# One Mamba-and-FFN block on one core: the first up and gate tile of a round ahead of the transposition of y's first half, in the last chunk and the tail

## Chip, core and metric

One core of a Trainium2 chip runs the whole kernel. The metric is the device time of one execution in microseconds (us); lower is better. The engines are TensorE (PE), VectorE (DVE), ScalarE (ACT), GpSimd (POOL) and SyncE (SP, which issues the DMAs here). Each runs its own list of instructions in order, and they meet at semaphores.

## What is computed

4096 tokens (4 sequences of 1024), 512 wide, float32:

```python
x = x + layernorm(mamba(layernorm(x)))
x = x + layernorm(ffn(layernorm(x)))

# mamba: DI = 1024 channels, 16 states, dt rank 128
hidden, gate = split(x @ W_in + b_in)
conv  = silu(causal_conv4(hidden) + conv_b)
dt, B, C = split(conv @ W_x)
delta = softplus(dt @ W_dt + b_dt)
h[t]  = exp(delta[t] * A) * h[t-1] + delta[t] * conv[t] * B[t]
y[t]  = sum over the 16 states of h[t] * C[t]
y     = (y + conv * d_param) * silu(gate)
out   = y @ W_out + b_out

# ffn: 2048 inner; fwht is a Hadamard transform with signs and scales
z   = silu(fwht(x) @ W_gate) * (fwht(x) @ W_up)
out = fwht(z) @ W_down
```

## The kernel before

The tokens are cut into NCH = 16 chunks of T = 256. The Hadamard transforms are folded into the FFN weights during the first chunks. The program is a pipeline over rounds c = 0 to 18. In round c four or five chunks are in work: `cur` = c is scanned, `front` = c + 1 gets its in_proj, convolution and delta, `back` = c - 1 has its y turned, gated and projected, `ff` = c - 2 goes through the FFN, and `fold` = c - 3 finishes it. A chunk that does not exist is `None`: at c = 15 there is no `front`, and at c = 16 neither `front` nor `cur`. At c = 17 there is no `back` either.

A round has 32 slots, two (tb = 0, 1) for each of the 16 states n. Every engine has its own hand-written `slot` or `in_slot` function, which lists what it issues in slot k; `run` calls it for all c and k. The order of work on an engine is thus written out by hand, and semaphores do the rest.

What PE issues around the change, in `in_slot` (L779):

- slot 0: `turn_h(back, 15, 0)`, then `up_gate(fold, 15)`;
- slot 1: `turn_f(ff)` (transposes of the FFN's input; ACT and DVE split the result into `fxT_hi` and `fxT_lo`), at c = 16 a `down`, then `turn_h(back, 15, 1)`;
- slot 2: `turn_y(back, 0)`, `up_gate(ff, 0)`, and with a `cur` `turn_h(cur, 0, 0)`;
- slot 3: `turn_y(back, 1)`, and with a `cur` `turn_h(cur, 0, 1)` and a `down`;
- from slot 4 on: one `turn_h` in each slot (with a `cur`), `up_gate` in the even ones, and `down` (FFN down projection, L742), `out_proj` of `back` (L703) and `in_proj` of the gate (L651) between them.

`turn_h` (L628, transposes L633), `turn_f` (L610, L615), `turn_x` and `turn_y` (L618, transposes L625) all write the one PSUM tile `hT`. Each starts with `begin_t` (L575), which waits until the use before it in the list `T_SEQ` (L185) has been read out: for a turn_h that is DVE's addition to `acc` (`add_h`, L1183; L1190 for n = 0, L1193 otherwise), for a turn_y DVE's `skip` (L1196; four instructions at L1200 which add `hT` to `conv`, `y_skip`). `turn_y(back, 0)` also waits for the last `acc` of `back`.

`up_gate(j, ft)` (L709, 24 matmuls at L726) makes the gate and up rows of FFN tile ft of chunk j. It waits for its weights (`ug_in` or `ug_kept`), for ft = 0 for `fx_lo`, and for the tile before it in the same PSUM bank:

```python
def gate_up_bank(no):
    return da[0] if no >= SPARE and no % 2 else pF
def bank_users(no):
    return no - 1 if no > SPARE else no
# in up_gate, no = j * HT + ft, HT = 16, SPARE = 224:
    if no:
        pe.wait_ge(p_done, bank_users(no))
```

`p_done` is counted up by the second instruction of DVE's `silu_up` (L1210; L1215 and L1217). The tiles of the rounds meant here are no = 208 (c = 15) and no = 224 (c = 16), and both use `pF`.

DVE's list around it, in its own `in_slot` (L1232), for a round with a `cur`:

- slot 1: scan(0, 2), `f_low` (`fxT_lo`), scan(0, 3), `add_h(back, 15, 1)`, `silu_up(fold, 15)`;
- slot 2: scan(1, 0), `skip(back, 0)`, scan(1, 1), `add_h(cur, 0, 0)`;
- slot 3: scan(1, 2), `skip(back, 1)`, scan(1, 3), `add_h(cur, 0, 1)`, `silu_up(ff, 0)`.

Here scan(n, q) is quarter q of state n (L1180). Without a `cur` the scans and the additions of `cur` are not there. ACT makes each quarter's `decay` (L986) when the scan two quarters back is done, the tanh (L1010), and once a round `gate_silu` (L1003), each use of which loads two activation tables, its own and then that of the next `decay`. POOL makes `dbx` (L1362), the low part of the product (`prod_lo`, L1426), the gating (L1410) and the last addition of a chunk (`xr`, L1436); SP's `store_out` waits for the latter, and SP's later loads stand behind it.

Of the kernel before, what the change touches and what calls it, by code (L numbers as in the profile page):

```python
# [35 lines left out]
def fused_block(nc, x, W, scratch_bc, scratch_ug, scratch_wd, out):  # L36
# [31 lines left out]
    with ctx:  # L68
# [108 lines left out]
        def chunk(c):  # L177

            return c if 0 <= c < NCH else None
# [7 lines left out]
        for c in range(LAST + 1):  # L187
            cur, front, back, ff = chunk(c), chunk(c + 1), chunk(c - 1), chunk(c - 2)
# [30 lines left out]
# [8 lines that stand above are left out]
        def kept(no):  # L227

            j, ft = divmod(no, HT)
            if j >= NCH - 2 and ft in KEPT:  # L230
                return KEPT.index(ft)
            return 0 if second_use(no) else None

        def second_use(no):

            return no == HT * NCH - 2
# [6 lines left out]
        def ug_tile(no):  # L243
            return wug[RING_NO[no] % 2] if kept(no) is None else kept_ug[kept(no)]
# [324 lines left out]
        def _(pe):  # L569
# [32 lines left out]
            def turn_x(j):  # L602
                pe.wait_ge(xn_done, TB * (j + 1))
                begin_t(("x", j, 0))
                for kt in range(KT):
                    for tb in range(TB):
                        mm = pe.transpose(hT[:, kt * T + tb * P:kt * T + (tb + 1) * P], xb[:, tb, kt * P:(kt + 1) * P], ident[:, :])
                mm.then_inc(x_turned, 1)

            def turn_f(j):  # L610
                pe.wait_ge(fn_done, TB * (j + 1))
                begin_t(("f", j, 0))
                for kt in range(KT):
                    for tb in range(TB):
                        mm = pe.transpose(hT[:, kt * T + tb * P:kt * T + (tb + 1) * P], ob[:, tb, kt * P:(kt + 1) * P], ident[:, :])  # L615
                mm.then_inc(fx_turned, 1)

            def turn_y(j, i):  # L618
                if i == 0:
                    pe.wait_ge(acc_done, NST * TB * (j + 1))  # L620
                begin_t(("y", j, i))
                for a in range(DT // 2):
                    dt = DT // 2 * i + a
                    for tb in range(TB):
                        mm = pe.transpose(hT[:, a * T + tb * P:a * T + (tb + 1) * P], acc[j % 2][:, tb, dt * P:(dt + 1) * P], ident[:, :])  # L625
                mm.then_inc(y_turned, 1)

            def turn_h(j, n, tb):  # L628
                if tb == 0:
                    pe.wait_ge(scan_done, NQ * (NST * j + n + 1))  # L630
                begin_t(("h", j, TB * n + tb))
                for dt in range(DT):
                    mm = pe.transpose(hT[:, dt * P:(dt + 1) * P], h[n % 2][:, dt, tb * P:(tb + 1) * P], ident[:, :])  # L633
                mm.then_inc(h_turned, 1)
# [74 lines left out]
            def up_gate(j, ft):  # L709
                no = j * HT + ft  # L710
                if kept(no) is None:
                    pe.wait_ge(ug_in[RING_NO[no] % 2], 16 * (RING_NO[no] // 2 + 1))
                else:
                    pe.wait_ge(ug_kept[kept(no)], 32 if second_use(no) else 16)
                if ft == 0:
                    pe.wait_ge(fx_lo, 2 * (j + 1))
                if no:
                    pe.wait_ge(p_done, bank_users(no))
                else:
                    pe.wait_ge(had_lo, NTILE)  # L720
                if no == SPARE + 1:
                    pe.wait_ge(scan_done, NQ * NST * NCH)
                for which in (1, 0):
                    for kt in range(KT):
                        for i, (a, b) in enumerate(PASSES):
                            mm = pe.matmul(gate_up_bank(no)[:, which, :], ug_tile(no)[:, 2 * which + a, kt, :], fxT[b][:, kt, :],  # L726
                                           start=(kt == 0 and i == 0), stop=(kt == KT - 1 and i == len(PASSES) - 1))
                mm.then_inc(ug_mm, 1)

            def down(j, ft):  # L730
                no = j * HT + ft
                if kept(no) is None:
                    pe.wait_ge(wd_in[RING_NO[no] % 2], 16 * (RING_NO[no] // 2 + 1))
                else:
                    pe.wait_ge(wd_kept[kept(no)], 32 if second_use(no) else 16)
                pe.wait_ge(p_lo, no + 1)
                if ft == 0 and j:
                    pe.wait_ge(z_evac, TB * j)
                split = (prod_hi[no % 2], prod_lo[no % 2])
                for tb in range(TB):  # L740
                    for i, (a, b) in enumerate(PASSES):
                        mm = pe.matmul(pD[tb][:, :], split[a][:, tb * P:(tb + 1) * P], wd_tile(no)[:, b, :],  # L742
                                       start=(ft == 0 and i == 0), stop=(ft == HT - 1 and i == len(PASSES) - 1))
                    if no == NCH * HT - 1:
                        mm.then_inc(last_down, 1)
                if no < NCH * HT - 1:
                    mm.then_inc(down_mm, 1)
# [31 lines left out]
            def in_slot(c, k, cur, front, back, ff, fold):  # L779
                n, tb = divmod(k, 2)  # L780
                if k == 0:
                    if front is not None:
                        turn_x(front)
                    if fold is not None:
                        down(fold, HT - 3)
                    if back is not None:
                        turn_h(back, NST - 1, 0)
                    if fold is not None:
                        up_gate(fold, HT - 1)
                    return  # L790
                if k == 1:
                    if ff is not None:
                        turn_f(ff)
                    if cur is None and fold is not None:
                        down(fold, HT - 2)
                    if front is not None:
                        in_proj("hid", front, *PE_HID[0])
                    if back is not None:
                        turn_h(back, NST - 1, 1)
                    if front is not None:  # L800
                        in_proj("hid", front, *PE_HID[1])
                    return
                if k in (2, 3):
                    if back is not None:
                        turn_y(back, k - 2)
                    if ff is not None and k == 2:
                        up_gate(ff, 0)
                    if front is not None and k == 3:
                        in_proj("hid", front, *PE_HID[3])
                    if cur is not None:  # L810
                        turn_h(cur, 0, tb)
                    if front is not None and k == 2:
                        in_proj("hid", front, *PE_HID[2])
                    if cur is not None and fold is not None and k == 3:
                        down(fold, HT - 2)
                    return
                if cur is not None:
                    turn_h(cur, n - 1, tb)
                if c == 1:
                    hadamard(c, k)  # L820
                if ff is not None and k in UG_SLOT:
                    up_gate(ff, UG_SLOT[k])
                if front is not None and k in PE_HID:
                    in_proj("hid", front, *PE_HID[k])
                if back is not None:
                    out_proj(back, PE_OUT.get(k, ()))
                if cur is not None and k in PE_GATE:
                    in_proj("gate", cur, *PE_GATE[k])
                if front is not None:
                    x_proj(front, PE_XPROJ.get(k, ()))  # L830
                if ff is not None and k in DOWN_SLOT:
                    down(ff, DOWN_SLOT[k])
                if fold is not None and k in DOWN_LATE:
                    down(fold, DOWN_LATE[k])
                if front is not None:
                    if k == 23:
                        turn_rows(front)
                    if k in PE_DT:
                        dt_proj(front, PE_DT[k])
# [712 lines left out]
```

## Time and profile before

| | us |
|---|---|
| median of 3 runs | 2653.99 |
| lowest and highest | 2649.32, 2655.06 |
| the profiled execution, its own time | 2655.23 |
| span of its trace | 2653.4 |
| PE busy | 2576.0 (97% of the span) |
| DVE busy | 2241.5 (84%) |
| POOL busy | 2044.5 (77%) |
| ACT busy | 1817.0 (68%) |
| mean DMA rate | 213 GB/s |

The profile is one execution. "Busy" counts time in which an instruction of the engine runs. Matmuls overlap, so a row's length can reach past the start of the next one; the distance between starts is what one costs. "Idle before" in brackets is how long the engine had stood still, and the arrow names the engine, the tile and the line that let it go. The granted clock is a share of TensorE's full 2.4 GHz; 0.50 is its lower level, 1.2 GHz. Two rounds matter here: the seat of c = 15 lies at about 2334 to 2354 us of the span, that of c = 16 at 2484 to 2496.

### The profile page before, as it was taken

What the parts mean: (1) busy time and instruction counts of PE and PEld (TensorE: products, weight loads), DVE (VectorE), ACT (ScalarE), POOL (GpSimd) and SP (SyncE); (2) the same over time, 40 slices, a digit from 0 to 9 for tenths busy, and PEclk for the clock granted to TensorE, in tenths of its full rate; (3) what the DMA queues carried; (4) which work ended last, traced back from release to release, by engine and by line L of the source; (5) the groups of instructions that cost most, each with busy time, mean ns of one, the idle gap of its engine ahead of it and who ended that gap; (6) DMA issues with size and microseconds to landing.
All of it is one profiled execution on the core that took longest, in us unless ns stands there. A gap on an engine that the chain in (4) does not pass through costs nothing.

```text
span 2653.4 us, 46296 instructions
## 1 busy us (share of the span) xinstructions
PE 2576.0 (97%) x16048; PEld 2187.0 (82%) x16048; DVE 2241.5 (84%) x2573; ACT 1817.0 (68%) x3935; POOL 2044.5 (77%) x1691
## 2 busy tenths in 40 slices
PE   7999989999999999999999999999999999989998
PEld 5566568989888888989888898988888898978888
DVE  6897998899888889898889889898889889889522
ACT  4776777677777777777777767777777777755322
POOL 6776879788787979888797978888797988877222
PEclk9999999999999999999999999999999999989999
DMA  5664246656666665766666665766666666646665
GB/s 181 205 212 167 100 156 208 227 205 234 217 224 227 216 223 198 238 212 227 222 217 224 214 226 197 242 210 236 217 217 221 208 223 214 223 175 230 263 266 186
DMA packets 165209, 564.41 MB, mean 213 GB/s; under 512 B 17264, under 2 KB 19696, under 8 KB 132976
## 3 DMA queue, kind: packets, MB, share of 16 engines
q1 hardware_dynamic: 164976, 561.44, 61.4%
q8 instruction: 129, 2.11, 0.3%
q14 instruction: 104, 0.85, 0.1%
HBM read 527.30 MB, written 34.08 MB: 212 GB/s over the span
## 4 chain that ended last, share of the span: by engine, by line
PE 77%; DVE 11%; ACT 7%; issue 3%; DMA 1%; POOL 0%; SPq 0%; DVEq 0%; ACTq 0%; POOLq 0%
PE pF L726 21%; PE hT L633 14%; PE pM L651 13%; PE pD L742 10%; PE pM L703 8%; DVE h L1180 6%; DVE acc L1193 3%; PE pM L673 3%; PE pD L766 2%; ACT decay L986 2%; PE decay L726 2%; PE hT L625 1%; PE pF L766 1%; ACT delta L963 1%; ACT delta L958 1%
## 5 line engine op out<-in xcount | busy, mean ns | idle before, releaser
L1180 DVE TENSOR_TENSOR_SCAN h<-decay,dbx 128x512 f32<-128x512 f32 x1024 | 1201.2, 1206 | 92.8 <-ACT decay L986 64.4
L1362 POOL TENSOR_TENSOR dbx<-u,bb 128x2048 f32<-128x2048 f32 (+1 forms) x272 | 1179.2, 4336 | 37.6 <-DVE h L1180 35.6
L986 ACT ACTIVATE decay<-delta,a_neg 128x255 f32<-128x255 f32 x2048 | 875.9, 468 | 315.5 <-DVE h L1180 308.7
L1193 DVE SCALAR_TENSOR_TENSOR acc<-hT,bcT,acc 128x1024 f32<-128x1024 f32 x480 | 610.0, 1271 | 122.5 <-PE hT L633 118.9
L726 PE MATMUL pF<-fxT_hi,wug 128*128 128x256 f32 x3632 | 709.9, 288 | 0.4 <-issue 0.4
L633 PEld LDWEIGHTS hT<-ident,h 128*128 128x128 f32 x4096 | 472.9, 141 | 144.2 <-issue 88.4
L726 PEld LDWEIGHTS pF<-fxT_hi,wug 128*128 128x128 f32 x3632 | 582.9, 192 | 0.9 <-issue 0.9
L633 PE MATMUL hT<-ident,h 128*128 128x128 f32 x4096 | 535.8, 274 | 36.1 <-DVE acc L1193 24.9
L726 PE MATMUL pF<-fxT_lo,wug 128*128 128x256 f32 x1816 | 514.3, 283 | 0.0
L651 PE MATMUL pM<-xnT,w_in 128*128 128x256 f32 x2016 | 480.4, 382 | 3.4 <-ACT hid L906 1.9
L651 PEld LDWEIGHTS pM<-xnT,w_in 128*128 128x128 f32 x2016 | 367.7, 192 | 51.1 <-issue 5.0
L1426 POOL TENSOR_TENSOR prod_lo<-prod,prod_hi 128x256 fp32r<-128x256 f32 x256 | 187.2, 731 | 279.3 <-ACT prod_hi L1017 278.6
L742 PE MATMUL pD<-wd,prod_hi 128*128 128x512 f32 x972 | 350.6, 442 | 3.0 <-POOL prod_lo L1426 2.0
L726 PEld LDWEIGHTS pF<-fxT_lo,wug 128*128 128x128 f32 x1816 | 349.2, 192 | 0.0
L1419 POOL TENSOR_TENSOR conv<-conv,tap 128x256 f32<-128x256 f32 x360 | 261.3, 731 | 27.3 <-ACT tap L932 8.5
L703 PE MATMUL pM<-w_out,gate 128*128 128x512 f32 x512 | 240.4, 593 | 0.5 <-DVE ob L1153 0.3
L742 PEld LDWEIGHTS pD<-wd,prod_hi 128*128 128x128 f32 x972 | 176.4, 189 | 59.2 <-issue 30.5
L742 PE MATMUL pD<-wd,prod_lo 128*128 128x512 f32 x486 | 192.0, 395 | 0.0
L1010 ACT ACTIVATE th<-pF,half_gate 128x256 f32<-128x256 f32 x240 | 111.9, 466 | 97.4 <-PE pF L726 95.6
L932 ACT ACTIVATE tap<-hid,taps 128x256 f32<-128x256 f32 x360 | 155.6, 497 | 0.0
L703 PEld LDWEIGHTS pM<-w_out,gate 128*128 128x128 f32 x512 | 88.7, 191 | 68.1 <-issue 66.0
L1215 DVE SCALAR_TENSOR_TENSOR prod<-th,pF 128x256 f32<-128x256 f32 x240 | 98.7, 411 | 51.7 <-ACT th L1010 51.7
(173 smaller groups left out, 2719.6 us busy)
## 6 DMA issues: line engine op xcount, KB each, us to landing
wug<-scratch_ug SPq DMA_DIRECT2D x243, 1024.0 KB, 4.8
wd<-scratch_wd SPq DMA_DIRECT2D x243, 512.0 KB, 4.1
w_in<-in_W_in SPq DMA_DIRECT2D x252, 256.0 KB, 2.9
bb<-scratch_bc SPq DMA_DIRECT2D x128, 256.0 KB, 4.6
xb<-in_hidden_states SPq DMA_DIRECT2D x16, 512.0 KB, 5.2
xr<-in_hidden_states SPq DMA_DIRECT2D x16, 512.0 KB, 5.8
out<-xr SPq DMA_DIRECT2D x15, 512.0 KB, 3.6
kept_ug<-scratch_ug SPq DMA_DIRECT2D x7, 1024.0 KB, 8.2
```

The costliest lines, as they stand in the source:

```text
L633: mm = pe.transpose(hT[:, dt * P:(dt + 1) * P], h[n % 2][:, dt, tb * P:(tb + 1) * P], ident[:, :])
L651: mm = pe.matmul(pM[:, a, :], w[:, kt, :], xnT[j % 2][:, kt, :], start=(kt == 0), stop=(kt == KT - 1))
L703: mm = pe.matmul(o, gate[:, dt, tb * P:(tb + 1) * P], w_out[:, dt, :], start=(dt == 0), stop=(dt == DT - 1))
L726: mm = pe.matmul(gate_up_bank(no)[:, which, :], ug_tile(no)[:, 2 * which + a, kt, :], fxT[b][:, kt, :], start=(kt == 0 and i == 0), stop=( ...
L742: mm = pe.matmul(pD[tb][:, :], split[a][:, tb * P:(tb + 1) * P], wd_tile(no)[:, b, :], start=(ft == 0 and i == 0), stop=(ft == HT - 1 and ...
L932: e = act.activation(tap[dt % 2][:, k, :], hid[:, dt, k:k + T], ACT.Copy, scale=taps[:, dt, k:k + 1])
L986: e = act.activation(da[q % 2][:, i, 1:], delta[c % 2][:, dt, 1:], ACT.Exp, scale=a_neg[:, dt, n:n + 1])
L1180: dve.tensor_tensor_scan(row(h[n % 2][:, tiles, :]), row(da[q % 2][:, :, :]), row(dbx[n % 2][:, tiles, :]), 0.0, ALU.mult, ALU.add).then_i ...
L1193: dve.scalar_tensor_tensor(acc[c % 2][:, tb, :], hT[:, :], cn, acc[c % 2][:, tb, :], ALU.mult, ALU.add).then_inc(acc_done, 1)
L1362: pool.tensor_tensor(dbx[n % 2][:, tiles, :], u[:, tiles, :], rows, ALU.mult).then_inc(done if restarts(c) else prod_done, 1)
L1419: pool.tensor_tensor(conv[j % 2][:, dt, :], conv[j % 2][:, dt, :], tap[dt % 2][:, k, :], ALU.add).then_inc(tap_added, 1)
L1426: pool.tensor_tensor(prod_lo[no % 2][:, :], prod[no % 2][:, :], prod_hi[no % 2][:, :].bitcast(F32), ALU.subtract).then_inc(p_lo, 1)
```

## The change

In slot 2 of PE's list, when there is no `front`, `up_gate(ff, 0)` is issued ahead of `turn_y(back, 0)` and not behind it. With a `front` the order stays. Nothing else is changed: no instruction is added or removed, and no other engine's list is touched. Since slot 2 needs both a `back` and an `ff` for the order to matter, two rounds are affected, c = 15 and c = 16.

```diff
                 if k in (2, 3):
+                    if front is None and ff is not None and k == 2:
+                        up_gate(ff, 0)
                     if back is not None:
                         turn_y(back, k - 2)
-                    if ff is not None and k == 2:
+                    if front is not None and ff is not None and k == 2:
                         up_gate(ff, 0)
                     if front is not None and k == 3:
                         in_proj("hid", front, *PE_HID[3])
```

## Rows read from the trace of the kernel before

**Rows 1.** The page: shares of the chain that ended last, by engine.

```profile
PE 77%; DVE 11%; ACT 7%; issue 3%; DMA 1%; POOL 0%; SPq 0%; DVEq 0%; ACTq 0%; POOLq 0%
```

**Rows 2.** PE's timeline at c = 15: start us, us, instructions [idle before <-releaser].

```profile
2336.62 1.83 PE L633 MATMUL hT<-ident,h 128*128 128x128 f32 x8 [2.01 <-DVE fxT_lo L1207]
...
2339.92 1.94 PE L625 MATMUL hT<-ident,acc 128*128 128x128 f32 x8 [1.47 <-DVE acc L1193]
...
2341.51 0.56 PE L726 MATMUL pF<-fxT_hi,wug 128*128 128x256 f32 x1
...
2342.09 0.63 PE L726 MATMUL pF<-fxT_hi,wug 128*128 128x256 f32 x2
...
2342.73 0.63 PE L726 MATMUL pF<-fxT_hi,wug 128*128 128x256 f32 x2
...
2345.40 1.04 PE L633 MATMUL hT<-ident,h 128*128 128x128 f32 x8
...
2347.82 1.09 PE L625 MATMUL hT<-ident,acc 128*128 128x128 f32 x8 [1.38 <-DVE acc L1190]
...
2350.66 1.97 PE L633 MATMUL hT<-ident,h 128*128 128x128 f32 x8 [1.75 <-DVE conv L1200]
```

**Rows 3.** PE's timeline at c = 16.

```profile
2485.50 1.10 PE L633 MATMUL hT<-ident,h 128*128 128x128 f32 x8 [0.62 <-DVE fxT_lo L1207]
...
2488.07 1.06 PE L625 MATMUL hT<-ident,acc 128*128 128x128 f32 x8 [1.47 <-DVE acc L1193]
...
2488.89 0.36 PE L726 MATMUL pF<-fxT_hi,wug 128*128 128x256 f32 x1
...
2491.84 1.04 PE L625 MATMUL hT<-ident,acc 128*128 128x128 f32 x8
```

**Rows 4.** PE's timeline: turn_y(0) at c = 14, a later turn_h.

```profile
2188.31 1.06 PE L625 MATMUL hT<-ident,acc 128*128 128x128 f32 x8 [0.17 <-DVE acc L1193]
...
2370.85 1.88 PE L633 MATMUL hT<-ident,h 128*128 128x128 f32 x8 [2.52 <-DVE acc L1193]
```

**Rows 5.** DVE's timeline at c = 15.

```profile
2338.49 1.28 DVE L1193 SCALAR_TENSOR_TENSOR acc<-hT,bcT,acc 128x1024 f32<-128x1024 f32 x1 [0.80 <-PE hT L633]
...
2340.13 0.42 DVE L1217 TENSOR_TENSOR prod<-pF,prod 128x256 f32<-128x256 f32 x1
...
2341.90 1.65 DVE L1200 SCALAR_TENSOR_TENSOR conv<-conv,d_skip,hT 128x256 f32<-128x256 f32 x4 [0.21 <-PE hT L625]
...
2343.47 1.22 DVE L1180 TENSOR_TENSOR_SCAN h<-decay,dbx 128x512 f32<-128x512 f32 x1
...
2354.66 2.33 DVE L1180 TENSOR_TENSOR_SCAN h<-decay,dbx 128x512 f32<-128x512 f32 x2
```

**Rows 6.** DVE's timeline at c = 16: the second instruction of silu_up(13, 15).

```profile
2488.28 0.42 DVE L1217 TENSOR_TENSOR prod<-pF,prod 128x256 f32<-128x256 f32 x1
```

**Rows 7.** Busy us of PE, PEld, DVE, ACT, POOL; then granted clock, DMA.

```profile
2343.00:2344.00 1.00, 1.00 (x8) 1.00 (x8) 1.00 (x3) 0.00 (x0) 0.77 (x2) 0.69 0.04 16
...
2355.00:2371.00 16.00, 12.27 (x90) 10.87 (x89) 15.90 (x19) 9.51 (x22) 13.73 (x8) 1.00 0.77 274
...
2371.00:2433.00 62.00, 62.00 (x373) 51.31 (x373) 54.66 (x61) 31.29 (x73) 42.07 (x30) 0.97 0.58 201
...
2484.00:2496.00 12.00, 9.91 (x78) 9.16 (x77) 7.39 (x15) 5.32 (x9) 0.74 (x1) 1.00 0.86 340
```

**Rows 8.** ACT's timeline at c = 15.

```profile
2344.72 0.87 ACT L986 ACTIVATE decay<-delta,a_neg 128x255 f32<-128x255 f32 x2 [2.13 <-DVE h L1180]
...
2350.84 1.81 ACT L986 ACTIVATE decay<-delta,a_neg 128x255 f32<-128x255 f32 x4
```

**Rows 9.** What PE waited for, 2480 to 2653.4: total us, times, longest.

```profile
PE pD L742 <- DMA wd<-scratch_wd: 1.0, 1, 1.0
PE decay L726 <- DMA wug<-scratch_ug: 0.5, 1, 0.5
```

## The prediction

> **What bounds the kernel now.** I read the page first for its totals: TensorE (PE) holds 77% of the chain that ended last, VectorE (DVE) 11% [rows 1]. So time is lost wherever PE stands still in the part that the change touches, or where DVE is the bound there and is held up. The diff touches two places only, as it asks for `front is None` and for `back` and `ff` to exist: slot 2 of c = 15 (the last chunk) and slot 2 of c = 16 (the first round of the tail). In c = 17 there is no `back`, so nothing moves. Next I read PE's timeline at the two places, then DVE's, and last what stands downstream.
>
> At c = 15 PE waits four times: 2.01 us for `fxT_lo`, 1.47 us for the last `acc` of the old chunk, 1.38 us for the first `acc` of the new one, 1.75 us for `conv` [rows 2]. At c = 16 it waits 0.62 and 1.47 us and then goes straight on [rows 3]. At c = 14, which has a front, the same transposition waits 0.17 us only [rows 4], since pieces of in_proj stand ahead of it. In the two touched rounds that cover is absent.
>
> **What the moved tile waits for.** The order is turn_y(0), up_gate(ff, 0) and becomes up_gate(ff, 0), turn_y(0). The 1.47 us are turn_y's, for the `acc` addition that DVE ends at 2338.49 + 1.28 = 2339.77 [rows 5]. up_gate needs its weights and `fx_lo` (turn_h ahead of it has waited for that already), and `p_done` of the tile before it, ft 15 of the chunk before, as both use bank pF. DVE's program has that silu_up behind the `acc` addition: it ends at 2340.13 + 0.42 = 2340.55 [rows 5], and at c = 16 at 2488.28 + 0.42 = 2488.70 [rows 6]. So the tile that is put first is free later than the transposition that it passes, by 0.78 us at each place. The gap isn't filled; it grows from 1.47 to about 2.25 us.
>
> **What the cover was for.** All transpositions write hT, so the one behind turn_y(0) waits for DVE's skip(0), four instructions, 1.65 us [rows 5]. Now up_gate lies between: turn_h(15, 0, 0) of c = 15 follows it at 2345.40 without a wait, and turn_y(1) of c = 16 at 2491.84 without one [rows 2, 3]. With the change skip is exposed at both. The trace prices that: where turn_h(15, 0, 1) stands right behind turn_y(1), PE waits 1.75 us for `conv` [rows 2].
>
> **Sum at c = 15.** up_gate is let go at 2340.55 + 0.15 (what PE took after the `acc` addition, 2339.77 to 2339.92) = 2340.70. At the full clock a matmul of it takes 0.12 us (24 of them, 2488.89 to 2491.84, with the next group's start 0.07 behind [rows 3]); at the lower level, 1.2 GHz, three take 2342.09 to 2342.73, so 0.213 each [rows 2]. The granted clock rises about 0.62 into the microsecond from 2343 (mean 0.69 between 0.5 and 1.0 gives 0.62 us low [rows 7]), so at 2343.6. From 2340.70 that makes 13.7 slow matmuls and 10.3 x 0.12 = 1.2 us: 2344.9. turn_y(0) ends 1.04 later, 2345.9; skip takes 0.05 + 1.65: 2347.6. turn_h starts at 2347.65 instead of 2345.40: **2.25 us late**. On DVE scan(1, 1) is queued behind skip: it runs from 2347.6 instead of 2343.47 [rows 5] and ends at 2348.75, as turn_h's result arrives; the next `acc` is 2.3 us late and not more.
>
> **Sum at c = 16.** 2488.70 + 0.15 = 2488.85; 24 x 0.12 = 2.88 gives 2491.73; transposes 1.04, skip 0.05 + 1.65, release 0.05: 2494.5 instead of 2491.84, **2.7 us late**.
>
> **What else stands behind the waits.** Both functions issue matmuls only; no DMA is moved, and nothing is moved past a queue of SP or GpSimd (POOL). On ScalarE (ACT) the `decay` of quarter 3 waits for scan(1, 1), and gate_silu with two table loads stands behind it. That quarter starts at 2348.8 instead of 2344.72, 4.1 later, so the next `decay` at 2354.9 instead of 2350.84, and its first half is there at 2355.8 [rows 8]; the scan that reads it stood at 2354.66 [rows 5] and now stands at 2357.0. Cover 1.2 us; without it the excess would add to the sum. At c = 16 up_gate(2) waits for silu_up(0), which comes behind skip(1). Both move with turn_y(1), and by the same sum silu_up ends at about 2498.1, some 1.7 us before PE gets there. Tile 0's tanh comes 0.2 us to 0.7 us earlier, for which nobody waits: worth nothing.
>
> **Does it pass downstream?** From 2355 to 2371 DVE is busy 15.90 of 16 us, then PE all 62 us to 2433 [rows 7]; both are behind the seat by data and order, so nothing takes 2.3 us up. Behind c = 16 PE waits for DMA for 1.0 and 0.5 us in all [rows 9]; SP issues these loads behind PE's progress and behind store_out, which waits for POOL and so for PE. I take full passage. The waits together: 2.25 + 2.7 = 4.95 us.
>
> **The clock term.** What came before a lower level: waits of 2.01 us, of 1.38 and 1.75 us, and of 2.52 us; after the last turn_h took 1.88 instead of 1.04 us [rows 2, 4]. What didn't: 0.62 and 1.47 us at c = 16, where the granted clock stays 1.00 [rows 3, 7]. The new wait there, about 2.2 us, is longer than the one of 2.01, and 1.8 us for skip follow, so I expect a low stretch at c = 16 that was not there. Its price from c = 15: the start of turn_y to the start of up_gate 1.59 us against 0.82, up_gate 3.89 against 2.95, together 1.7 us [rows 2, 3]; some of it will fall into a wait, so I take 1.5. Bounds: 3.4 (one more at both places, all on the path), 0 (none), and a gain of up to 1.6, if the low stretch at 2370.85 (0.8 us in turn_h and as much in the up_gate behind it) falls into a wait instead.
>
> The trace at c = 16 shows that from 2485.50 to 2488.89 PE ran nothing but sixteen transposes around a wait, at a clock of 1.00 [rows 3, 7]. The Trainium skill ("TensorE: Matmul & The Clock Gate", Part 4: PE-mode transpose) says that transposes don't count as activity for the clock; the stretch doesn't confirm it, nor rule it out. By that rule the new c = 15, where transposes alone run from 2344.9 to about 2354, would be sure of a low stretch more, and the result would be that of rival 4.
>
> **Forecast.** 2.25 + 2.7 + 1.5 = 6.45 us. The profiled execution took 2655.23 us (span 2653.4), 1.24 above the median 2653.99 of three. Profiled 2661.7; median 2660.4, which is +0.24%. What a measurement of this kernel can tell from no change is about 0.2%, 5.3 us.
>
> **Rivals.** (1) *The waits, and no clock term*: 4.95 us, 2658.9, +0.19%: not slower by the bound. For it: 1.38 us and 1.47 us waits left the level where it was, and where the drop sets in between 1.5 and 2.0 us the rows don't tell. It decides if c = 16 keeps 1.00 through a 2.2 us wait. (2) *Part is taken up behind c = 16*: PE's waits for `wd` and `wug`, 1.5 us [rows 9], vanish if these loads keep their time when PE is late; with or without the clock term that leaves 3.4 to 4.9 us, 2657.4 to 2658.9, not slower. Against it: the order of SP's queue. (3) *The intended gain*: up_gate free right behind turn_h. At c = 16 it would start at 2486.4, and 2.88 + 1.04 + 1.75 us later it is 2492.1, still 0.2 behind 2491.84; at c = 15, all at the lower level, some 0.9 behind: 2655. Against it: bank pF and DVE's order. Faster than before takes the favour of the clock on top, 2652. (4) *The clock falls at both places*: 4.95 + 3.4 = 8.4 us, 2662.3; with ACT's cover gone 2664.
>
> **Chances.** Forecast 0.50 (its own range 2659 to 2662.5), (1) 0.24, (2) 0.08, (3) 0.05, (4) 0.13. Slower: 0.63, less 0.03 that the scatter puts under the bound, 0.60. Faster 0.03, out of (3); within 0.2%: 0.37. The range, 2656 to 2664.5, takes in (1), (2) and nearly all of (4), and a scatter of a median by 1 us.
>
> **What would show it.** At both places: up_gate released by DVE `prod` L1217 after 2.1 to 2.3 us of wait; turn_y(0) without a wait; 1.7 to 1.9 us of wait for `conv` L1200 ahead of turn_h(15, 0, 0) and of turn_y(1); turn_h 2.25 us later than 2345.40; from there to the end the same distances, but for a low stretch at c = 16. Wrong if up_gate starts with the `acc` release (`p_done` wasn't late), if skip's wait is under 1 us, if the distance from turn_y(1) of c = 16 to the end shrinks by over 0.5 us (rival 2), or if c = 16 keeps its clock (rival 1).

## The result and the profile after

| | before | after |
|---|---|---|
| median, us | 2652.37 (11 runs; the 3 known ahead gave 2653.99) | 2660.21 (11 runs) |
| lowest and highest | 2649.32, 2655.06 | 2655.75, 2662.81 |
| ratio to before | | 1.0026, 95% interval 1.0018 to 1.0034 |
| profiled execution, own time | 2655.23 | 2661.83 |
| its span | 2653.4 | 2660.0 |

The change makes the kernel slower by 7.8 us at the median, 4.8 to 9.0 by the interval. The two profiled executions differ by 6.6 us. In one run of a version tried below (`e8_best`) the granted clock was 0.556 and the time 4380.36 us; the figures for that version are of its other ten runs.

PE's timeline of the changed kernel at c = 15, the rows that answer to [rows 2]. DVE's and ACT's line numbers are two higher than before.

```profile
2336.42 1.80 PE L633 MATMUL hT<-ident,h 128*128 128x128 f32 x8 [2.01 <-DVE fxT_lo L1209]
2340.47 0.55 PE L726 MATMUL pF<-fxT_hi,wug 128*128 128x256 f32 x1 [2.25 <-DVE prod L1219]
...
2344.74 1.04 PE L625 MATMUL hT<-ident,acc 128*128 128x128 f32 x8
2347.62 1.07 PE L633 MATMUL hT<-ident,h 128*128 128x128 f32 x8 [1.84 <-DVE conv L1202]
2350.06 1.78 PE L625 MATMUL hT<-ident,acc 128*128 128x128 f32 x8 [1.38 <-DVE acc L1192]
2353.59 1.97 PE L633 MATMUL hT<-ident,h 128*128 128x128 f32 x8 [1.75 <-DVE conv L1202]
```

Read the brackets from top to bottom. The 2.01 us wait is the old one. Then up_gate waits 2.25 us for `prod`, where turn_y(0) had waited 1.47 us for `acc`. turn_y(0) has no wait, and turn_h(15, 0, 0), which had none, now waits 1.84 us for `conv`. The last two waits are the old ones.

The same at c = 16, answering to [rows 3]:

```profile
2488.40 1.09 PE L633 MATMUL hT<-ident,h 128*128 128x128 f32 x8 [0.62 <-DVE fxT_lo L1209]
2491.75 0.36 PE L726 MATMUL pF<-fxT_hi,wug 128*128 128x256 f32 x1 [2.25 <-DVE prod L1219]
...
2494.70 1.04 PE L625 MATMUL hT<-ident,acc 128*128 128x128 f32 x8
...
2497.49 1.09 PE L625 MATMUL hT<-ident,acc 128*128 128x128 f32 x8 [1.75 <-DVE conv L1202]
```

DVE's timeline at c = 15, to be held against [rows 5]:

```profile
2338.26 1.28 DVE L1195 SCALAR_TENSOR_TENSOR acc<-hT,bcT,acc 128x1024 f32<-128x1024 f32 x1 [0.76 <-PE hT L633]
2339.46 0.41 DVE L1217 SCALAR_TENSOR_TENSOR prod<-th,pF 128x256 f32<-128x256 f32 x1
2339.90 0.42 DVE L1219 TENSOR_TENSOR prod<-pF,prod 128x256 f32<-128x256 f32 x1
...
2345.82 1.66 DVE L1202 SCALAR_TENSOR_TENSOR conv<-conv,d_skip,hT 128x256 f32<-128x256 f32 x4 [4.36 <-PE hT L625]
2347.39 1.22 DVE L1182 TENSOR_TENSOR_SCAN h<-decay,dbx 128x512 f32<-128x512 f32 x1
2348.72 1.28 DVE L1192 TENSOR_SCALAR acc<-hT,bcT 128x1024 f32<-128x1024 f32 x1
```

silu_up ends at 2340.32 and PE's up_gate starts 0.15 us later. skip had waited 0.21 us for its transposes and now waits 4.36 us, and DVE stands still behind it.

Where the 6.6 us of the profiles arise is seen by the distance of each mark from the turn_h that waits for `fxT_lo` at c = 15 (2336.62 before, 2336.42 after; these 0.20 us are why the last line has 6.80 and not 6.6):

| mark on PE | before | after | grown by |
|---|---|---|---|
| turn_h(15, 0, 0) | 8.78 | 11.20 | 2.42 |
| turn_h(15, 0, 1) | 14.04 | 17.17 | 3.13 |
| turn_h(15, 15, 1) of c = 16 | 148.88 | 151.98 | 3.10 |
| turn_y(1) of c = 16 | 155.22 | 161.07 | 5.85 |
| end of the span | 316.78 | 323.58 | 6.80 |

The first seat costs 2.42 us, 0.7 us come right behind it, nothing is given back in the 135 us from there to c = 16, the second seat costs 2.75 us, and 0.95 us come later.

Busy times and clock by stretch. The first row is of the kernel before, a stretch not shown ahead. Its 0.85 is the mean granted clock over 46 us.

```profile
2334.00:2380.00 46.00, 35.66 (x215) 31.08 (x214) 40.37 (x51) 26.83 (x54) 35.29 (x22) 0.85 0.52 189
```

And after:

```profile
2334.00:2380.00 46.00, 33.15 (x201) 29.27 (x200) 38.26 (x48) 23.95 (x49) 32.41 (x20) 0.81 0.48 172
...
2358.00:2374.00 16.00, 12.38 (x92) 11.01 (x91) 15.87 (x19) 9.50 (x22) 13.74 (x8) 1.00 0.79 277
2374.00:2436.00 62.00, 62.00 (x374) 51.31 (x373) 54.74 (x60) 31.29 (x73) 42.04 (x30) 0.97 0.58 200
2487.00:2500.00 13.00, 8.37 (x66) 7.45 (x65) 6.36 (x13) 4.97 (x7) 0.74 (x1) 1.00 0.79 313
```

The time at the lower level (0.5) is twice what the mean lacks: 0.15 x 2 x 46 = 13.8 us before, 0.19 x 2 x 46 = 17.5 us after, each good to half a us, as the means are rounded. The added piece is where turn_y(1) takes 1.78 in place of 1.09 us: that is the 0.7 us behind the first seat. DVE is again the full engine for 16 us, then PE for 62, each 3 us later than in [rows 7]. At c = 16 the clock stays 1.00.

### The profile page after: what moved, and what is told of

Same layout as the page of the kernel before. It is cut to its first block, busy times and chain, and to the rows that moved or that the text cites. A ratio compares the mean times of both kernels' runs of the same rounds, so it can differ in the third digit from the quotient of the medians.

```text
span 2660.0 us, 46296 instructions
## 1 busy us (share of the span) xinstructions
PE 2576.7 (97%) x16048; PEld 2187.3 (82%) x16048; DVE 2241.7 (84%) x2573; ACT 1817.0 (68%) x3935; POOL 2044.7 (77%) x1691
## 4 chain that ended last, share of the span: by engine, by line
PE 77%; DVE 11%; ACT 7%; issue 3%; DMA 1%; POOL 0%; SPq 0%; DVEq 0%; ACTq 0%; POOLq 0%
PE pF L726 21%; PE hT L633 14%; PE pM L651 13%; PE pD L742 10%; PE pM L703 8%; DVE h L1182 5%; DVE acc L1195 3%; PE pM L673 3%; PE pD L766 2%; ACT decay L988 2%; PE decay L726 2%; PE hT L625 1%; PE pF L766 1%; ACT delta L965 1%; ACT delta L960 1%
```

## The experiments

Times are medians of 11 runs (5 where said). Ratios are to runs of the kernel before on the same chips. A difference "at equal clock" comes from a straight line through each kernel's runs, time against their mean granted clock, read at 0.996. The slope is 1.1 to 2.5 us for each 0.001; for the kernel before (its 87 runs in the comparisons below) it is 1.7 us, and its mean clock is 0.9964, that of the changed kernel 0.9952. The clocks are known to 0.001 only, so such a line is rough. The diffs are cut to the lines that matter.

**One place at a time.** `e1_only15` has the new order at c = 15 only, `e2_only16` at c = 16 only. Each is shown by its first condition against the changed kernel's; the condition behind turn_y is the opposite one:

```diff
-                    if front is None and ff is not None and k == 2:
+                    if front is None and cur is not None and ff is not None and k == 2:   # e1
+                    if cur is None and ff is not None and k == 2:                         # e2
```

> The new order at c = 15 only. Theory (two longer or bared waits, each passed on whole): PE waits 2.3 us for `prod` L1219-like ahead of up_gate and 1.8 us for `conv` ahead of turn_h(15,0,0); that seat is 2.3 us late and one more low-clock stretch behind it can add 0.8 to 1.6 us; c = 16 has the rows of before (waits 0.6 and 1.5 us). Total +2.3 to +4 us on before. Rival 'the loss is a matter of the clock only': the total follows the granted clock and is +3 us or more only where the clock is below that of before. Rival 'c = 16 makes all of it': 0 to +1 us.

> The new order at c = 16 only. Theory: waits of 2.3 us (prod) and 1.75 us (conv) there, turn_y(1) 2.7 us late, c = 15 as before; total +2.7 us, up to +4.5 where the clock falls at c = 16. If the two places add up, this and the kernel with c = 15 only make the 7.8 us of the full change (+-1.5). Rival 'taken up behind c = 16 by the waits for weights': +1 us or less.

Measured: e1 2656.68 us, ratio 1.0019 (1.0010 to 1.0027); e2 2657.19 us, 1.0018 (1.0009 to 1.0028). PE in e1, the c = 15 and the c = 16 seat:

```profile
2337.87 0.55 PE L726 MATMUL pF<-fxT_hi,wug 128*128 128x256 f32 x1 [2.25 <-DVE prod L1219]
...
2345.12 1.07 PE L633 MATMUL hT<-ident,h 128*128 128x128 f32 x8 [1.84 <-DVE conv L1202]
...
2488.28 1.06 PE L625 MATMUL hT<-ident,acc 128*128 128x128 f32 x8 [1.47 <-DVE acc L1195]
```

PE in e2:

```profile
2338.57 1.94 PE L625 MATMUL hT<-ident,acc 128*128 128x128 f32 x8 [1.47 <-DVE acc L1195]
...
2487.65 0.36 PE L726 MATMUL pF<-fxT_hi,wug 128*128 128x256 f32 x1 [2.26 <-DVE prod L1219]
...
2493.39 1.09 PE L625 MATMUL hT<-ident,acc 128*128 128x128 f32 x8 [1.75 <-DVE conv L1202]
```

Each place has its own pair of waits and leaves the other alone. At equal clock e1 is 2.2 us and e2 2.8 us above the kernel before, together 5.0, and the full change is 5.3 us above it: the two places add up, and each has the size of its waits. The plain medians (+5.0, +5.5) are higher and their sum too large for the full change; with intervals of about +-2.4 us each they do not say more. Neither place is empty, and c = 16's loss isn't taken up by the waits for weights behind it.

**The wait for `p_done`.** `e3_silu_first_after` is the changed kernel with DVE's silu_up earlier, `e5_silu_first_before` the kernel before with the same move:

```diff
+                    if front is None and fold is not None:      # slot 1, behind f_low
+                        silu_up(fold, HT - 1)
                 if cur is not None:
                     scan(cur, n, 2 * tb + 1)
...
-                if k == 1 and fold is not None:
+                if k == 1 and front is not None and fold is not None:
                     silu_up(fold, HT - 1)
```

> The changed kernel, with DVE's silu_up(fold, 15) moved ahead of scan(0, 3) and the last `acc` addition in rounds without a front, so that bank pF is free when turn_h(back, 15, 1) ends. Theory: up_gate starts without a wait, the acc wait is covered, only skip's 1.75 us stays bare; +0.2 us at c = 16 and +0.9 at c = 15 on before, total +1 us (0 to +2.5 with the clock). Rival 'the bared skip is the whole loss and p_done costs nothing': total stays +5 to +8 us.

> Control for the kernel with silu_up moved: the kernel before, with DVE's silu_up(fold, 15) ahead of scan(0, 3) and the last `acc` in rounds without a front, PE's order as before. Theory: nobody on PE waits for silu_up in this order, and scan(0, 3) still ends about when turn_h(15, 15, 1) does; 0 us (-0.5 to +0.5). Rival 'moving silu_up is itself what gained in the run before': -3 us or more.

Measured: e3 2651.55 us, 1.0001 (0.9992 to 1.0010); e5 2652.70 us, 1.0002 (0.9993 to 1.0011). PE in e3:

```profile
2337.61 0.56 PE L726 MATMUL pF<-fxT_hi,wug 128*128 128x256 f32 x1
...
2341.58 1.03 PE L625 MATMUL hT<-ident,acc 128*128 128x128 f32 x8
2344.45 1.07 PE L633 MATMUL hT<-ident,h 128*128 128x128 f32 x8 [1.84 <-DVE conv L1202]
...
2489.21 1.04 PE L625 MATMUL hT<-ident,acc 128*128 128x128 f32 x8
2492.00 1.09 PE L625 MATMUL hT<-ident,acc 128*128 128x128 f32 x8 [1.75 <-DVE conv L1202]
```

up_gate and turn_y(0) have no wait, the wait for skip is still there, and the whole loss is gone (at equal clock 0.4 us are left). So PE's new order is harmless once bank pF is free in time: what it gains in the `acc` wait, it pays back at skip (at c = 16 from turn_h to turn_y(1) 6.62 us, against 6.34 before and 9.09 after). e5 shows that the DVE move by itself gains nothing.

**The cover for skip at c = 16.** `e4_cover16` is the changed kernel with up_gate(ff, 1) ahead of turn_y(1):

```diff
+                    if cur is None and back is not None and k == 3:   # and no longer in slot 4
+                        up_gate(ff, 1)
                     if back is not None:
                         turn_y(back, k - 2)
```

> The changed kernel, with up_gate(ff, 1) ahead of turn_y(1) at c = 16, so that skip(0) is covered again there. Theory: the 1.75 us wait for `conv` goes, PE's next tile there is 0.8 us late in place of 2.75, total 1.9 us less than the changed kernel, about +6 us on before. Rival 'the wait for skip hides something else that is late anyway (gate_silu, gating)': the wait returns as another one before out_proj and the total stays +7.8 us.

Measured: 2658.93 us, 1.0027 (1.0018 to 1.0036), 1.3 us under the changed kernel; at equal clock 1.5 us under. PE:

```profile
2494.73 1.04 PE L625 MATMUL hT<-ident,acc 128*128 128x128 f32 x8
...
2498.40 0.35 PE L726 MATMUL pF<-fxT_hi,kept_ug 128*128 128x256 f32 x1 [1.24 <-DVE prod L1221]
```

The wait for `conv` is gone, but 1.24 us come back in front of up_gate(2): it needs silu_up(0), which DVE's list has behind skip(1), and skip(1) follows turn_y(1). The expectation's theory missed this; its rival had a wait come back, but a different one. From turn_h to up_gate(2) the distance is 13.71 us, against 14.28 after (2488.40 to 2502.68) and 11.48 before. The time is too scattered to tell 0.6 from 1.9 us; the trace says 0.6.

The same trace shows something of the clock. At c = 15 this kernel has the order and the waits of the changed one, but there the first turn_h still runs at the full clock, turn_y(1) too (1.09 us against 1.78), and the mean over the 46 us is 0.85 and not 0.81:

```profile
2334.00:2380.00 46.00, 35.66 (x212) 30.70 (x213) 39.05 (x50) 24.80 (x51) 32.33 (x22) 0.85 0.52 187
```

So where the lower level falls, and how long it lasts, differs between two executions with the same instructions and waits at c = 15.

**The clock.** Matmuls that nobody reads fill PE's waits, so that the granted clock need not fall. They go into pM, which is idle there:

```python
def fill(use, count):
    begin_m(use)
    for i in range(count):
        pe.matmul(pM[:, 0, :], ident[:, :], xnT[0][:, 0, :], start=True, stop=True)
```

> The kernel before, with matmuls that nobody reads (128x256 float32 into pM, about 0.22 us each) in PE's waits at c = 15 (7 ahead of turn_h(14, 15, 1), 5 ahead of turn_y(0), 5 ahead of turn_y(1), 6 ahead of turn_h(15, 0, 1), 8 ahead of turn_h(15, 3, 1)'s successor in slot 8) and at c = 16 (5 ahead of turn_y(0)). All are shorter than the wait that they lie in. Theory: the granted clock keeps 1.00 at both places, the waits stay as they were less the filling, and the low stretches' share goes: -2 to -3.5 us on before (turn_y 0.8, up_gate 0.9, turn_h of slot 8 and the tile behind it 1.6). Rival 'the low clock of c = 15 costs nothing, as DVE binds there': 0.

> The same in the changed kernel (7; 8 ahead of up_gate(0), 6 ahead of turn_h(15, 0, 0), 5, 6 and 8 at c = 15; 8 and 6 at c = 16). Theory: without low stretches the difference between the two orders is the waits alone, 2.3 + 2.7 = 5 us on the filled kernel before; so this is at +2 to +3 us on the plain kernel before. Rival 'the clock is the whole difference': equal to the filled kernel before within 1 us. Rival 'the waits passed on cost more than their length': 7 us or more between the two filled kernels.

Measured: e6 2650.51 us, 0.9996 (0.9987 to 1.0005); e7 2661.98 us (5 runs), 1.0040 (1.0027 to 1.0052). Both miss, by my mistake. The filling for up_gate's wait in e7:

```profile
2337.05 3.62 PE L778 MATMUL pM<-xnT,ident 128*128 128x256 f32 x16
```

Eight matmuls of float32 are sixteen rows and 3.6 us, twice what I had counted, in a wait of 2.25 us. These fillings lengthen what they should only fill, so the difference of e6 and e7 tells nothing about the orders. With counts that fit:

> The filled kernel before again, with fillings that fit: a float32 matmul nobody reads takes 0.43 us (two passes of 0.22), not 0.22, so the counts are now 4, 3, 3, 3 and 5 at c = 15 and 3 at c = 16 (1.7, 1.3, 1.3, 1.3, 2.2, 1.3 us in waits of 2.0, 1.47, 1.38, 1.75, 2.5, 1.47). Theory: no low-clock stretch at c = 15, DVE's times as before; mean clock 0.998 or more; 2 to 3.5 us less than before. Rival 'the low clock there costs nothing': 0.

> The filled changed kernel with counts 4, 4, 3, 3, 3, 5 at c = 15 and 4, 3 at c = 16, all shorter than their waits. Theory: the difference to the filled kernel before is the waits alone, 2.3 + 2.7 = 5 us (4.5 to 6); the rest of the 7.4 us between the unfilled ones, some 2 us, was the clock. Rival 'the waits cost more than their length': 7 us or more between the filled ones. Rival 'all is clock': 1 us or less.

Measured: e9 2648.43 us, 0.9984 (0.9975 to 0.9993), mean clock 0.9979; e10 2652.61 us, 1.0006 (0.9997 to 1.0015), mean clock 0.9983. The stretch from 2334 to 2380 in e9 and then in e10:

```profile
2334.00:2380.00 46.00, 43.19 (x284) 36.08 (x283) 44.88 (x55) 28.49 (x60) 36.76 (x25) 1.00 0.57 207
```

```profile
2334.00:2380.00 46.00, 42.57 (x277) 35.68 (x276) 42.47 (x52) 26.51 (x55) 34.40 (x23) 1.00 0.54 189
```

The low stretches of c = 15 are gone in both. Without them the orders differ by 4.2 us in the medians and 4.9 us in the means, against 7.8 (medians) and 7.3 us (means) unfilled. By the runs the waits are thus some 5 us and the clock some 2 to 3 us, but each difference has an interval of about +-2 us, so the clock's part is hardly clear of nothing.

The traces put most of the loss on the waits. Measured from the turn_h that waits for `fxT_lo`, on PE:

| mark | e9 | e10 | grown by | unfilled, for comparison |
|---|---|---|---|---|
| turn_h(15, 0, 0) | 6.34 | 9.17 | 2.83 | 2.42 |
| turn_h(15, 0, 1) | 11.59 | 14.45 | 2.86 | 3.13 |
| turn_h(15, 15, 1) of c = 16 | 143.98 | 146.83 | 2.85 | 3.10 |
| turn_y(1) of c = 16 | 150.32 | 155.92 | 5.60 | 5.85 |

At the full clock the two orders are 5.60 us apart at the last mark, against 5.85 with the low stretches: in these traces the clock adds 0.25 us. Where the rest of the 2 to 3 us of the runs comes from, they do not show. In e10 the waits are still there in full. What its rows show as wait is what the filling leaves: 0.53 us for `prod` behind four matmuls of 0.43 makes 2.26, 0.54 us for `conv` behind three makes 1.84:

```profile
2335.90 0.35 PE L726 MATMUL pF<-fxT_hi,wug 128*128 128x256 f32 x1 [0.53 <-DVE prod L1234]
...
2341.72 1.07 PE L633 MATMUL hT<-ident,h 128*128 128x128 f32 x8 [0.54 <-DVE conv L1217]
```

Filling alone takes some 4 us off the kernel before (1.9 to 6.6 by the interval), more than I had expected of it. The traces bear it out. From the start of turn_f (L615) of c = 15, ahead of which nothing is changed, to the end it is 319.8 us in the kernel before and 314.8 in e9, 5.0 us less. Ahead of it the executions scatter by themselves: turn_f starts at 2329.51 us in e10 and at 2335.18 in e5.

**Versions that keep both covers.** `e8_best` has silu_up first as in e3. At c = 15 it puts the gate half of up_gate(ff, 0) ahead of turn_y(0) and the up half behind. At c = 16 it puts tile 0 in bank da[0], which needs no `p_done` of the last tile (so `bank_users` asks for one less), and tile 1 in pF. The wait for the last scan, which reads da[0], moves from tile 1 to tile 0:

```diff
-            return da[0] if no >= SPARE and no % 2 else pF
+            return da[0] if no >= SPARE and no % 2 == 0 else pF
...
-            return no - 1 if no > SPARE else no
+            return no - 1 if no >= SPARE else no
...
+                    if cur is None and back is not None:
+                        up_gate(ff, k - 2)
+                    if front is None and cur is not None and k == 2:
+                        up_gate(ff, 0, 1)
                     if back is not None:
                         turn_y(back, k - 2)
+                    if front is None and cur is not None and k == 2:
+                        up_gate(ff, 0, 0)
```

`e11_best_fill` adds fillings of 4, 3, 3 and 5 matmuls at c = 15.

> A version that keeps both covers. silu_up(fold, 15) first as above; at c = 15 up_gate(ff, 0) cut in two: gate half ahead of turn_y(0), up half behind it; at c = 16 up_gate(ff, 0) in the free bank da[0] ahead of turn_y(0) and up_gate(ff, 1) in pF between the two turn_y. Theory: at c = 16 no wait of 1.47 us and none for skip, 1.5 us less than before; at c = 15 turn_y(0) up to 0.8 us later at the low clock, but turn_h(15, 0, 0) right behind skip, 1.3 us earlier; total -2.8 us on before (-1.5 to -4). Rival 'the slots behind have their own bound, the gain is given back': within 0.5 us of before.

> The version that keeps both covers, with fillings of 4, 3, 3 and 5 at c = 15. Theory: its gain on before (1.4 to 2.2 us) and what the low stretches cost it (1 to 2 us) add up: -2.5 to -4 us on before, about 2649. Rival 'fillings or covers hold up something else': no better than the version without fillings (-1.8 us).

Measured: e8 2649.84 us (10 runs), 0.9992 (0.9983 to 1.0001); e11 2648.78 us, 0.9987 (0.9978 to 0.9996). PE in e8:

```profile
2340.32 1.04 PE L625 MATMUL hT<-ident,acc 128*128 128x128 f32 x8
...
2343.19 1.07 PE L633 MATMUL hT<-ident,h 128*128 128x128 f32 x8 [0.41 <-DVE conv L1212]
...
2486.12 1.04 PE L625 MATMUL hT<-ident,acc 128*128 128x128 f32 x8
...
2489.87 1.04 PE L625 MATMUL hT<-ident,acc 128*128 128x128 f32 x8
2493.54 0.36 PE L716 MATMUL decay<-fxT_hi,kept_ug 128*128 128x256 f32 x1 [1.23 <-DVE prod L1229]
```

At c = 15 turn_y(0) has no wait and the one for skip is 0.41 us (0 before, 1.84 after); at c = 16 both waits are gone, but 1.23 us return ahead of up_gate(2) for the reason seen in e4. The gain of 2.1 us is at the edge of what the runs can tell, and not all of it is cover: c = 15 has less of the lower level, a mean of 0.93 over the 46 us where the kernel before has 0.85. With fillings the version is faster than before, but not than the kernel before with fillings (e9): from turn_f to the end it is 314.6 us in e11 and 314.8 in e9. At the full clock the covers bring 0.2 us, so cover and filling do not add up as I expected.

## Why the prediction was right

**What the moved tile waits for** held to the hundredth: released by `prod` after 2.25 us at both places, 0.78 us later than the transposition would have been. e3 shows that the loss hangs on this term: without this wait it is gone.

**Skip bared** held: 1.84 and 1.75 us of wait for `conv`, predicted 1.7 to 1.9.

**The sum at c = 15** was 2.25 us, the trace has 2.42. Of the rest, 0.09 is the wait for skip, 1.84 us against the 1.75 of my sum. The next `acc` starts at 2348.72, 0.11 us after scan(1, 1) ends and 0.03 us after turn_h does, so the scan queued behind skip adds nothing, as worked out. **At c = 16** it was 2.7 and is 2.75. At equal clock the two places measure 2.2 and 2.8 us, and the full change 5.3 against 4.95. At the full clock the seat of c = 15 costs more, 2.83 us (e9 to e10).

**ACT's cover** held: the next `decay` starts at 2354.74 (forecast 2354.9). The scan that reads it came at 2357.59.

**Full passage downstream** held in chunk 15 (3.13 us at its start, 3.10 at its end). Behind c = 16 the profile has 0.95 us more, of which 0.65 us are waits for weights: 0.46, 0.84 and 0.88 us instead of 0.53 and 1.00:

```profile
2553.97 0.73 PE L742 MATMUL pD<-kept_wd,prod_hi 128*128 128x512 f32 x2 [0.46 <-DMA kept_wd<-scratch_wd]
...
2556.47 0.39 PE L726 MATMUL decay<-fxT_hi,wug 128*128 128x256 f32 x1 [0.84 <-DMA wug<-scratch_ug]
...
2574.65 0.73 PE L742 MATMUL pD<-wd,prod_hi 128*128 128x512 f32 x2 [0.88 <-DMA wd<-scratch_wd]
```

From turn_y(1) to the end is 161.6 us before and 162.5 after, but also 162.0 in e2, 162.7 in e1 and 164.3 in e5, whose PE order is the old one. So this piece scatters by itself, and I don't put it down to the change.

**The clock term** had the wrong place, and that its size was right is not shown. I forecast a low stretch at c = 16 at 1.5 us, since its new wait is longer than one of 2.01 us that went before a low level. In the traces of the changed kernel, e2 and e4, c = 16 keeps 1.00 through the wait of 2.25 us and the next of 1.75 (e4: 1.24). The added low time of the changed kernel and of e1 is at c = 15 (13.8 to 17.5 us), where the new wait for skip joins four others; e4, with the same waits there, does not have it. So a single wait was the wrong thing to compare, and what decides is open. As to the size, I forecast 1.5 us. The runs say 2 us by the lines at equal clock and 2 to 3 by the filled kernels, with an interval as wide as that. The traces find 0.7 us behind the first seat, but 0.25 in all up to turn_y(1) of c = 16 once the orders are compared filled. And e2's runs have a mean clock of 0.9954, as low as the changed kernel's, though its trace has at c = 15 and 16 the clock of before (0.85 and 1.00).

The Trainium skill says that transposes do not count as busy time for the clock as matmuls do ("TensorE: Matmul & The Clock Gate", Part 4: PE-mode transpose). This would have had the low stretch at c = 15, and there it came: from 2344.74 to 2355 PE runs transposes and waits only. But the waits there also add up to 5.0 us of some 10, and the fillings of e10, true matmuls, ended both at once. In e8 PE ran transposes and waits only from 2343.19 to 2349.32, and the clock stayed at 1.00. What the transposes had to do with it stays open; no run here separates it.

The criterion of rival 1 was met (no term at c = 16); its 2658.9 us lies 1.3 us under the median, which doesn't rule its size out. For the clock I took 1.5 us, about the middle of the bounds 0 and 3.4; the runs gave 7.8 us in all, and the interval of 4.8 to 9.0 holds 6.45, but also rival 1's 4.95 us and rival 4's 8.4. So what the runs bear out of the reasons is the waits and their passage. That the median of 2660.21 lies 0.2 us from the forecast 2660.4 is luck: the change cost 1.4 us more than forecast, and the kernel before, with more runs, came out 1.6 us lower. So, in part, is the profile (2661.83 against 2661.7): its 6.6 us are 5.85 us up to turn_y(1) of c = 16 and 0.95 us of scatter behind it, less 0.20 us of scatter ahead of c = 15; the forecast had 4.95 and 1.5.

## What to carry to other kernels

Before putting work into a gap, look up what that work itself waits for, and where the engine that releases it has that in its own list: here the tile was free 0.78 us later than what it was to precede. Then ask what the moved work had been covering. And where TensorE stands still several times in a few us, look at its granted clock: here matmuls that nobody reads, put into the waits, won more (4 us) than the best reordering (2.1 us).

## What the runs showed of the hardware

- The time of a run follows its mean granted clock by 1.7 us for each 0.001 (87 runs of the kernel before, 0.993 to 0.998, 2649 to 2660 us). My estimate from the span of 2653 us: 0.001 less is 5.3 us at the lower level, which costs 2.65 us where TensorE is the bound in all of it.
- At c = 16 a wait of 2.25 us, 4.0 us of work (2491.75 to 2495.74) and a wait of 1.75 us left the clock at 1.00; at c = 15 of the kernel before waits of 1.38 and 1.75 us with transposes between them were followed by the lower level [rows 2]. In e8 waits of 0.41, 1.38 and 1.75 us in the same place, transposes between them, left it at 1.00:

```profile
2342.00:2352.00 10.00, 6.39 (x46) 5.16 (x45) 9.74 (x15) 7.71 (x11) 4.86 (x5) 1.00 0.35 123
```

- A float32 matmul of 128x256 shows as two rows of 0.22 us, while one of the FFN's (fp32r) is one row of 0.12 us [rows 3].
